# A decoder layer on one core: the first layer's outputs two to a PSUM bank, its ring of matrices from five to nine, and the last low parts of the attention on VectorE

## The reference

```python
x = x + _L0_attn_ref(_layernorm(x), W_qkvb, W_o, ln_g, ln_b)        # fast-weight memory, 16 heads of 64
x = x + _L0_xattn_ref(_layernorm(x), ctx, Wq, Wk, Wv, Wout, bout)   # cross attention, 8 heads of 128
x = x + _L0_ffn_ref(_layernorm(x), router_w, w1, w2)                # 8 experts, one per token
```

## Time and profile before

| what | value |
|---|---|
| median of 3 runs | 1533.22 us (1531.67 to 1535.69) |
| the profiled execution: its own time | 1533.82 us |
| its span in the trace | 1532.0 us |
| PE matmul busy | 1354.0 us, 88% |
| DVE busy | 1118.5 us, 73% |
| ACT busy | 937.3 us, 61% |
| POOL busy | 894.0 us, 58% |

### The profile page before, as it was taken

One profiled execution on the slowest core, in us unless ns is written; L12 is line 12 of the kernel. 1 busy time (PEld: TensorE's weight loads), 2 busy tenths in 40 slices (PEclk: granted clock), 3 DMA queues, 4 the chain that ended last, 5 costly groups with the idle time before them and its releaser, 6 DMA issues. The chain is left out here.

```text
span 1532.0 us, 21903 instructions
## 1 busy us (share of the span) xinstructions
PE 1354.0 (88%) x7240; PEld 1109.8 (72%) x7240; DVE 1118.5 (73%) x1714; ACT 937.3 (61%) x1278; POOL 894.0 (58%) x537
## 2 busy tenths in 40 slices
PE   4999999696999479999999999999999999856797
PEld 3788887585788357777777777777777777646797
DVE  6789998546810368888888888988898888826354
ACT  3444433024654347887887877878888878633584
POOL 1310111113330248898998988989989889763553
PEclk9999999797999679999999999999999999985799
DMA  9102020007565247777777777777777767636572
GB/s 267 13 5 63 1 76 15 28 1 238 212 210 195 71 136 193 195 211 191 199 207 186 207 193 194 212 186 209 206 194 204 202 176 205 162 84 239 184 240 93
DMA packets 196444, 241.40 MB, mean 158 GB/s; under 512 B 58499, under 2 KB 101893, under 8 KB 196336
## 3 DMA queue, kind: packets, MB, share of 16 engines
q1 hardware_dynamic: 132032, 143.13, 32.6%
q10 hardware_dynamic: 62256, 91.04, 21.8%
q0 software_dynamic: 2048, 5.90, 1.0%
HBM read 64.79 MB, written 41.32 MB: 69 GB/s over the span
## 5 line engine op out<-in xcount | busy, mean ns | idle before, releaser
L1157 POOL TENSOR_TENSOR xa_pT<-xa_moved,xa_pT 128x1024 fp32r<-128x1024 f32 x256 | 609.3, 2401 | 55.4 <-ACT xa_pT L1253 54.5
L1184 PE MATMUL xa_S<-xa_kT,xa_qT 128*128 128x512 f32 x1536 | 405.9, 415 | 65.2 <-ACT xa_probs L1259 48.5
L1184 PEld LDWEIGHTS xa_S<-xa_kT,xa_qT 128*128 128x128 f32 x1536 | 291.6, 195 | 161.4 <-ACT xa_probs L1259 79.6
L1199 PE MATMUL xa_O<-xa_pT,xa_v 128*128 128x512 f32 x1536 | 375.0, 393 | 10.0 <-ACT xa_oT L1278 5.5
L1259 ACT ACTIVATE xa_probs<-xa_S,xa_nb 128x1024 f32<-128x1024 f32 x256 | 286.0, 1117 | 99.2 <-DVE xa_nb L1315 77.2
L1199 PEld LDWEIGHTS xa_O<-xa_pT,xa_v 128*128 128x128 f32 x1536 | 290.3, 190 | 74.3 <-POOL xa_pT L1157 7.4
L1325 DVE STREAM_TRANSPOSE xa_tq<-xa_probs 128x1024 f32<-128x1024 f32 x256 | 316.9, 1238 | 32.0 <-ACT xa_probs L1259 29.7
L1253 ACT ACTIVATE xa_pT<-xa_moved 128x1024 fp32r<-128x1024 f32 x256 | 269.8, 1060 | 83.3 <-issue 68.2
L1310 DVE TENSOR_REDUCE xa_mx<-xa_S 128x1 f32<-128x1024 f32 x128 | 155.8, 1217 | 113.7 <-PE xa_S L1184 112.7
L1312 DVE TENSOR_REDUCE xa_mxp<-xa_S 128x1 f32<-128x1024 f32 x128 | 157.6, 1231 | 22.0 <-PE xa_S L1184 17.0
L441 PE MATMUL fw_pp<-fw_hT,fw_wqk 128*128 128x512 f32 x384 | 100.8, 413 | 9.9 <-DVE fw_F L587 8.3
(11 more groups left out here) (199 smaller groups left out, 1762.9 us busy)
## 6 DMA issues: line engine op xcount, KB each, us to landing
xa_moved<-xa_tq SPq DMA_DIRECT2D x1024, 64.0 KB, 2.1
xa_moved<-xa_tq ACTq DMA_DIRECT2D x1024, 64.0 KB, 2.1
heads_k<-ci_outs SPq DMA_DIRECT2D x32, 256.0 KB, 2.0
heads_v<-ci_outs SPq DMA_DIRECT2D x32, 256.0 KB, 2.2
heads_q<-ci_outs SPq DMA_DIRECT2D x32, 256.0 KB, 2.0
xa_chunk<-heads_v ACTq DMA_DIRECT2D x32, 256.0 KB, 3.2
ex_w1s<-in_L_ffn_w_dram SPq DMA_DIRECT2D x8, 1024.0 KB, 7.2
ex_w2s<-in_L_ffn_w_dram SPq DMA_DIRECT2D x8, 1024.0 KB, 8.9
```

Source lines behind the costliest of these rows:

```text
L1157: pool.tensor_tensor(quadrants(pT[LO], r), unit_moved(r), quadrants(pT[HI], r).bitcast(F32), ALU.subtract).then_inc(lo_ready, 1)
L1184: last = pe.matmul(S[:, k], qT[a][:, i // GT % 2, q], kT[b][:, h % 2, k * 512:(k + 1) * 512], start=(n == 0), stop=(n == 2))
L1199: last = pe.matmul(O[:], v[a][:, j * P:(j + 1) * P], pT[b][:, r % PRING, k], start=(j == 0 and n == 0), stop=(j == JT - 1 and n == 2))
```

## The change

In the first layer output n goes to half a bank: bank pair by n // 2 and n // 4, half by n % 2, so that eight outputs have room where four had. out_project(n) waits for residuals only from n = 8 on, and then for pairs of them. residual(n) waits until both outputs of its bank are there. The ring has nine slots. Its slots 5 to 8 lie over tmp and over wv, which moves into the arena behind it, so the spreads 5 to 8 wait for the last projection of v (`v_mm`). VectorE makes its spreads among 16 to 21 ahead of residual 0 to 7 (16 to 20 before).

In the cross attention GpSimd's loop ends after slot 127, with the low parts of quarter 121. VectorE forms the twelve low parts of quarters 122 to 127 in slots 128 to 133, two to a slot, at the slot's end, so behind add_output and row_stats where the slot has them. Each waits for GpSimd's 244 low parts and for its high part.

```diff
-WRING = 5
+WRING, WFIRST = 9, 5
...
-                           ("DR", 4 * HG * BLKS * HN * CELL), ("tmp", 4 * 2 * 7 * GCOL), ("ebuf", 4 * 2 * 2 * CHUNK)):
+                           ("ebuf", 4 * 2 * 2 * CHUNK), ("DR", 4 * HG * BLKS * HN * CELL), ("tmp", 4 * 2 * 7 * GCOL),
+                           ("wv", 4 * 2 * DC * NH * DH)):
...
-        wv = [sb(f"fw_wv{i}", [P, DC, NH, DH], F32R) for i in (HI, LO)]
+        wv = [home(f"fw_wv{i}", "wv", [P, DC, NH, DH], F32R, i * 4 * DC * NH * DH) for i in (HI, LO)]
...
+        def output(n):
+
+            return gr[:, n // 2 % 2, n // 4 % 2, n % 2 * D:(n % 2 + 1) * D]
...
-            if m < WRING:
+            if m < WFIRST:
                 eng.wait_ge(dr_out, 16 * HALVES * (1 + 2 * HG))
+            elif m < WRING:
+                eng.wait_ge(v_mm, TILES)
             else:
                 eng.wait_ge(pv_mm, m - WRING + 1)
...
-                if n < 4:
+                if n < T:
                     pe.wait_ge(masked, 2 * PAIRS * UNITS)
                     pe.wait_ge(wo_in, 16)
                 else:
-                    pe.wait_ge(res_done, n - 3)
+                    pe.wait_ge(res_done, (n - T) // 2 * 2 + 2)
                 for c in range(INNER // P):
-                    last = pe.matmul(gr[:, n % 2, n // 2 % 2, 0:D], oT[:, c, t], wo[:, c],
+                    last = pe.matmul(output(n), oT[:, c, t], wo[:, c],
...
-                dve.wait_ge(y_mm, n + 1)
-                dve.scalar_tensor_tensor(hall[:, n], gr[:, n % 2, n // 2 % 2, 0:D], FAST_SCALE, hall[:, n],
+                dve.wait_ge(y_mm, n // 2 * 2 + 2)
+                dve.scalar_tensor_tensor(hall[:, n], output(n), FAST_SCALE, hall[:, n],
...
-            spread_units(PVS // 2, PVS // 2 + WRING)
+            spread_units(PVS // 2, PVS // 2 + 6)
             for n in range(T):
                 residual(n)
-            spread_units(PVS // 2 + WRING, PVS)
+            spread_units(PVS // 2 + 6, PVS)
...
+        LAST = SLOTS - LAG + 1
...
-            for s in range(SLOTS + LAG - 1):
+            for s in range(SLOTS):
                 p = s - LAG + 1
                 if p >= 0:
                     low_part(2 * p)
                     low_part(2 * p + 1)
-                for c in chunks_of(s) if s < SLOTS else []:
+                for c in chunks_of(s):
                     chunk_low(c)
...
+            def low_part(r):
+
+                dve.wait_ge(lo_ready, 2 * LAST)
+                dve.wait_ge(hi_ready, r + 1)
+                dve.tensor_tensor(quadrants(pT[LO], r), unit_moved(r), quadrants(pT[HI], r).bitcast(F32),
+                                  ALU.subtract).then_inc(lo_ready, 1)
...
                 if s < SLOTS:
                     transpose(s, 0)
+                elif s - LAG + 1 < SLOTS:
+                    for r in (0, 1):
+                        low_part(2 * (s - LAG + 1) + r)
```

## The result

The changed kernel takes 1516.66 us, the median of four runs (1515.30 to 1520.61); the kernel before takes 1534.45 in the same comparison. One of its four runs took 6487.01 us, far from all others; the ratio leaves it out, and without it the median is 1533.22. The ratio is 0.9894 with a 95% interval of 0.9866 to 0.9923. The forecast was 1513.8 us with a range of 1509 to 1520. The profiled execution took 1517.31 us, 16.5 less than that of before.

The account below looks back on a forecast made before the run. TensorE, busy 88% of the span, left only its gaps to be won. First layer 18.9 plus attention's end 0.5 made 19.4 us off 1533.8, so 1514.4 profiled; the median, 0.6 lower, 1513.8 us, range 1509 to 1520.

Parts of the forecast that it names:

- Combines 0 to 15: First layer: 16 combines without the 1.58 us wait, 14.3 us, as VectorE's spreads start earlier; gain 1.9 us.
- Outputs 0 to 7: First layer: eight outputs need no residual and take 27.9 us, ending at 286.7, not 306.0; gain so far 19.3 us.
- VectorE's path to combine 31: First layer, behind solve 3: four spreads, eight residuals, eight spreads, one collision, one combine; ends at 302.9 us, against 322.2.
- The last pair of residuals: First layer's end: residual 14 no longer runs beside output 15, so 0.35 us of the gain is lost.
- First layer: Whole first-layer part of the change: 18.9 us less, between 16.8 and 20.9.
- End of the attention: Last quarters of the attention, low parts on VectorE at 1.17 us each: 0.5 us less in all.
- rival B: Attention's end: TensorE idles some 2.3 us ahead of quarter 127, its clock falls; 2.1 us more, 1515.9 us; chance 0.10.
- The loop and the start: Attention loop stays as it is; the tiles' new places issue no instruction: no change in time.
- A: First layer: VectorE's solves, spreads and residuals cost more, 4.2 us come back, 1518.0 us; chance 0.13.
- C: Attention's end: ScalarE's issues run unhindered and the sum's copy comes 2.4 us earlier, 1511.4 us; chance 0.06.
- D: Attention loop: it meets VectorE late, 1.2 us per late slot, slower, 1542.6 us; chance 0.03.
- E: First layer: TensorE still waits, held by residuals or spreads through another semaphore; no gain, 1533 us; chance 0.03.

Follow-up runs that it names:

- the first part alone: New first layer with the old attention, against the kernel before: ratio 0.9875, and 0.9888 when run again (median 1516.13 us).

## Why the prediction was right, point by point

- *Combines 0 to 15.* Predicted 14.3 us in one piece, a gain of 1.9. Measured 14.19, a gain of 2.1. The ring alone showed the same piece.
- *Outputs 0 to 7.* Predicted 27.9 us at full clock with no gap; measured 27.89. This is the gain's main term: 15.6 us came with the banks alone.
- *VectorE's path to combine 31.* From the end of v it was predicted at 60.4 us (242.5 to 302.9); measured 59.9 (244.55 to 296.39 + 8.08). The terms: four spreads 4.62 against 4.65, eight residuals 2.74 against 2.8, eight spreads 11.11 against 9.3 + 2.05. That GpSimd's spreads would cost VectorE about the duration of one was right: two of them ran beside the eight, for some 2 us.
- *The last pair of residuals.* 0.35 us back: 0.76 behind output 15 against 0.42.
- *First layer.* Predicted 18.9 less, measured 19.4, and 19.6 with the first part alone.
- *End of the attention.* Predicted 0.5 less, measured 0.7 more, and 1.3 more in the mean of four traces. The low parts were right (1.18 us against 1.17), and so was the order that holds them. The last one came 1.1 us ahead of GpSimd's (40.94 and 42.08) and not 0.5, but in the mean of the traces only 0.1. What was mis-sized is the clock's term, which stood at nothing in the sum and at 2.1 us and one chance in ten as rival B. It came in three of four traces, at 1.6 us for the quarter. Its gap was 1.9 us and not 2.3. The prediction says that the rows show nothing for such a gap. Its rows don't, but the same timeline of the kernel before does, at quarter 123:

```profile
1342.68 4.60 PE L1199 MATMUL xa_O<-xa_pT,xa_v 128*128 128x512 f32 x12 [1.94 <-POOL xa_pT L1157]
```

Twelve matmuls took 4.60 us behind a gap of 1.94. Read beside the gap that the new order would open, this row spoke for rival B.
- *The loop and the start.* Put at nothing. The profiled execution lost 2.0 us ahead of the projections' end and 0.4 in the loop. With 1.2 at the attention's end, less 0.5 in the first layer and 0.1 behind the attention, all against the prediction, that makes up the difference between the 1514.4 us predicted for the profiled execution and its 1517.31. The 2.0 us at the start are also why the first layer ends at 333.9 us and not at 332 to 333. At least half of the first 2.0 looks like chance: the first part alone reached that point at 244.4 us in one execution and at 243.3 in another. But the eleven traces with the ring of nine reach it at 242.7 to 244.6, 243.4 in the mean, and the three with the ring of five at 242.4 to 242.9, 242.6 in the mean. Whether the new places of the tiles cost some 0.8 us of it stays open.
- *Rivals.* A did not come: VectorE's path to combine 31 was 0.5 us shorter than predicted. C's mechanism did come, though it is no effect of the change: the six issues ahead of the sum's copy took 3.81 us, and the copy came 1.7 us earlier than in the trace of before. In the four other traces with GpSimd's low parts they took 3.79 to 4.54 as well, so the 5.54 on which the prediction's path rested was one execution's. D and E are refuted by the first layer's rows and by a loop without a lasting shift. The range held the median. One of the four runs, 1520.61, lay above it.

## What to carry to other kernels

Before a faster engine takes over work at the end of a stage, write down what stands ahead of that work in its queue: here 2.36 us of low parts stood behind 2.64 us of outputs that nobody needed yet, and the order, not the engine, decided between 1.3 us lost and 1.7 us won. Where an engine waits for a buffer to be emptied by one that is busy with a long calculation, more room is worth the wait and the slow clock behind it, less what the engine then meets late: here 17.4 us and 15.6. Count banks by what fits in them. And where VectorE and GpSimd share a series of two-input operations, other work of VectorE at the point where GpSimd's result is due may be the safer order: the long wait came in one of three traces without it and in none of the eleven others. That is a count, not a test.

## What the runs showed that I had not expected

**GpSimd can be held off by VectorE altogether.** One GpSimd spread took 9.88 us beside the last seven of twelve spreads of VectorE back to back, and with the next one 11.80, against 4.92 for two in another execution of the same order and 2.05 for one alone. Times of GpSimd are rough in a profile, but TensorE's wait of 4.77 us for that spread confirms it. It is one of 112 GpSimd spreads in the fourteen traces; all others took 1.9 to 3.0 us. What decides between the two outcomes, the traces don't show. The Trainium skill (SBUF — State Buffer, on its two separate sides) says that the shared port pair is held for a whole instruction by whichever starts first, the other being blocked. The two rows agree with a lock, and show beyond that sentence that the waiting engine need not get its turn between two instructions of the other.

**The clock can fall behind a gap of 1.9 us**: ahead of quarter 127 in three of four traces the twelve matmuls behind it took 4.6 us, in the fourth 3.01. At the attention's end of all fourteen traces quarters 122, 123 and 127 have seventeen gaps of 1.90 to 1.97 us, the kernel before among them. Behind eleven the mean granted clock of the quarter was 0.63 to 0.65, behind six it stayed 1.00. Nor does the gap's length alone decide: it fell behind one of 2.27 and stayed behind two of 2.29. Filling the gap with work whose result nobody reads brought 3.04 back, and ahead of quarter 124 it brought 3.01 for 5.49.

**A stage of identical instructions varies more than the changes to the attention's end**: 972.0 to 979.6 us for the column called loop in fourteen traces.
